# A perceiver layer on one core: the second attention with its last softmax in two halves, contiguous K for the content, staging slots renumbered, and V projections, transposes and products regrouped

## The chip, the core and the metric

The kernel runs on one core of a Trainium2 chip. A core has four compute engines and DMA queues, each with a program of its own: TensorE (PE) multiplies matrices into the eight banks of PSUM, VectorE (DVE) and ScalarE (ACT) work element by element and copy results out of PSUM, GpSimd (POOL) does the same on SBUF alone, and SyncE (SP) issues the transfers between DRAM and SBUF. They wait for one another only by semaphores. The metric is the device time of one execution in microseconds (us); lower is better.

## What is computed

Queries are x, 4 batches of 128 rows of 512 values (16 heads of 32), and a context of 2048 rows per batch. Three residual blocks follow one another, each behind a layer norm: a cross attention over the context (softmax over heads and batches), a self attention with relative positions, and a third attention with normalised queries and gates. The change lies in the second:

```python
q, k, v = (proj(Wq), proj(Wk), proj(Wv))
a_q = Eq[rel]; a_k = Ek[rel]; a_v = Ev[rel]         # rel: clipped distance of l and m
content = jnp.einsum('bhld,bhmd->bhlm', q, k)
rel_k = jnp.einsum('bhld,lmd->bhlm', q, a_k)
rel_q = jnp.einsum('bhmd,lmd->bhlm', k, a_q)
pos_pos = jnp.einsum('lmd,lmd->lm', a_q, a_k)
logits = (content + rel_k + rel_q + pos_pos) * scale
attn = jax.nn.softmax(logits, axis=-1)
out = jnp.einsum('bhlm,bhmd->bhld', attn, v) + jnp.einsum('bhlm,lmd->bhld', attn, a_v)
```

All of it is float32. Projections are made of three products of rounded parts ("hi" and "lo"), twelve matmuls of 512 columns for one 128 x 512 result.

## The kernel before

The code is written by hand, engine by engine; the order in a function is the order on the engine, and every wait is written out. No scheduler moves anything.

The second attention works in four groups (`hg` or `u`, 0 to 3) of four heads, each over all four batches. For each group PE projects K (`keys2`) into bank 4 and Q (`queries2`) into bank 5, in two halves each, with the relative rows (`relative(n)`, 16 rounds, four a group: two for "rq", made of K, and two for "rk", made of Q) between them, in banks 0 to 3. ACT copies K and Q out of PSUM with row and batch exchanged (`k_lb`, `q_lb`: batch innermost, so that rows of all batches stand together for the relative products); one batch of `k_lb` is read with a step of four floats. DVE copies Q once more, contiguous (`q_rows`), from the same bank.

The relative rows are evacuated into six staging slots of the `blocks` buffer (`staged(n)`, DVE for rq, ACT for rk), stored by SP to DRAM (`rel_store`, 636 KB each) and read back with a skewed pattern that turns distances into columns (`rel_load`, 1210 KB each): `rq_in_u` and `rk_in_u`. SP's order is fixed: stores of the next group between the two loads of one. After them come the load of the third attention's Wq (`weight_load(4)`), of the table of values `EvRel`, and of its Wk (`weight_load(5)`, once POOL has done `weight_lo(4)`).

Then, for each group, PE writes the logits into banks 4 to 7: sixteen transposes of the rq part (L639) and sixteen matmuls of content over it (L644). DVE adds the rk part (`add2`, L1486) and takes maximum and difference (`softmax2`, L1490 and L1493); of group 3 it leaves the difference to ACT, which has the scaled maximum (L1496) as bias. ACT exponentiates (`exp2`; group 3 in sixteen instructions, L1078), PE transposes the probabilities (`attention_t(u)`, L663, groups 0 and 1 through banks 0 to 3, 2 and 3 through banks 4 to 7), and ACT (group 2: DVE, L1521) copies them into `probs_t(u)`, which shares the `blocks` buffer with the staging slots, so before the first of these copies ACT waits for all stores. V is projected by batch (`values2(b, bank)`, L381) through banks 0 and 1. PE multiplies attention and V (L704, sums in banks 0 to 3), ACT copies the results (L1115), PE puts them back transposed (L712), and the table of values follows in four banks of 64 matmuls' records (L724); DVE scales with the reciprocal sums and adds the residual (L1532, L1534), transposes the table part (L1540), POOL scales it (L1283), PE adds it (L741), and the third layer norm begins (`moments2`, square root on ACT at L873).

Weights of the third attention come in between: ACT rounds them (`weight_hi(n)`, L881) and POOL makes the low part (`weight_lo(n)`, L1217).

## Time and profile before

| | us |
|---|---|
| median of 3 runs | 748.01 |
| lowest and highest | 745.55, 748.47 |
| the profiled execution, its own time | 749.99 |
| its span | 748.0 |
| mean granted clock of PE | 0.993 |

The span is the time from the first to the last record of the profiled execution. Busy times of the page: PE 718.3, DVE 625.2, ACT 490.0, POOL 502.3 us. In the page's view in 40 slices, the DMA share of the slices between about 580 and 636 us is 9, and 4 or under nearly everywhere else behind the first slice. In this span the first attention lasts to about 567 us, the second from there to about 671, the third to the end. A busy share is a mean over these stages; each stage has limits of its own, and what a change in one is worth is read from the waits of that stage. "Idle before" in a row is the time in which the engine had nothing to do before it, and behind the arrow stands what released it; "issue" means that the profile shows no wait.

### The profile page before, as it was taken

Reading aid. Unit: us, or ns where it says so; the run is one execution under the profiler, and the core shown is the slowest. Engines: PE = TensorE matmul, PEld = TensorE weight load, DVE = VectorE, ACT = ScalarE, POOL = GpSimd, SP = SyncE. Lnnn points to the kernel's source line nnn. Section 1 sums busy time; section 2 is a strip of 40 time slices with the busy share of each in tenths; the row PEclk is TensorE's granted clock in tenths of the full one; section 3 lists DMA queues with packets and bytes.
Section 4 is the critical chain, followed back from the end, with each engine's and each line's share of the span. In section 5 each row is a group of like instructions: output and inputs, shape, how many; then the busy total and the mean of one; then the engine's idle time right before and its main releaser. Section 6 shows DMA issues by size and latency. Waiting matters only on the chain.

```text
span 748.0 us, 17289 instructions
## 1 busy us (share of the span) xinstructions
PE 718.3 (96%) x7542; PEld 572.1 (76%) x7542; DVE 625.2 (84%) x507; ACT 490.0 (66%) x694; POOL 502.3 (67%) x282
## 2 busy tenths in 40 slices
PE   8999999999999999999999999999988979889988
PEld 7777777777777777877778777787676667767876
DVE  5479999999999999999999999999946349767685
ACT  5578668777777867768677687767615444725681
POOL 0165979889898898989989898897962020243300
PEclk9999999999999999999999999999999999999999
DMA  8310110101101011010101101010013999420101
GB/s 330 115 58 6 53 57 2 58 1 58 57 2 58 1 58 39 19 58 3 57 7 53 57 2 58 1 58 2 1 57 112 337 391 362 172 100 1 57 2 57
DMA packets 15339, 55.71 MB, mean 74 GB/s; under 512 B 1696, under 2 KB 2080, under 8 KB 11680
## 3 DMA queue, kind: packets, MB, share of 16 engines
q1 hardware_dynamic: 15264, 54.61, 20.0%
q8 instruction: 60, 0.98, 0.6%
q14 instruction: 15, 0.12, 0.1%
HBM read 43.13 MB, written 11.47 MB: 73 GB/s over the span
## 4 chain that ended last, share of the span: by engine, by line
PE 81%; DVE 10%; ACT 5%; issue 3%; POOL 0%; ACTq 0%; DVEq 0%; POOLq 0%
PE ps L381 25%; PE ps L362 24%; PE ps L470 9%; PE ps L497 7%; PE ps L370 2%; PE ps L617 2%; PE ps L419 2%; DVE blocks L1476 1%; PE ps L724 1%; ACT v_buf L906 1%; DVE extra L1370 1%; DVE extra L1399 1%; DVE ps L1399 1%; PE ps L639 1%; PE ps L644 1%
## 5 line engine op out<-in xcount | busy, mean ns | idle before, releaser
L1239 POOL TENSOR_TENSOR s_buf<-s_buf,r_all 128x1024 f32<-128x1024 f32 x93 | 197.2, 2159 | 3.6 <-DVE r_all L1412 3.6
L930 ACT ACTIVATE s_buf<-s_buf 128x1024 f32<-128x1024 f32 x128 | 135.7, 1065 | 10.0 <-DVE s_buf L1392 9.1
L914 ACT COPY s_buf<-ps 128x1024 f32<-128x1024 f32 x128 | 123.3, 1018 | 20.4 <-PE ps L470 20.4
L1370 DVE TENSOR_REDUCE extra<-s_buf 128x128 f32<-128x2048 f32 x48 | 109.5, 2281 | 10.4 <-ACT s_buf L914 10.4
L1392 DVE TENSOR_TENSOR s_buf<-s_buf,ps 128x2048 f32<-128x2048 f32 x48 | 106.9, 2282 | 0.5
L1217 POOL TENSOR_TENSOR w_lo<-raw,w_hi 128x2048 fp32r<-128x2048 f32 x6 | 27.8, 4636 | 99.2 <-ACT w_hi L881 70.1
L906 ACT COPY v_buf<-ps 128x512 f32<-128x512 f32 x64 | 37.6, 588 | 77.5 <-PE ps L381 58.0
L1206 POOL TENSOR_TENSOR v_buf<-v_buf,extra 128x512 f32<-128x512 f32 x64 | 81.1, 1303 | 7.8 <-ACT v_buf L906 7.8
L1399 DVE TENSOR_REDUCE ps<-s_buf 128x128 f32<-128x4096 f32 x16 | 70.8, 4428 | 16.1 <-ACT s_buf L930 16.0
L1212 POOL TENSOR_TENSOR odd_lo<-extra,odd_hi 128x512 fp32r<-128x512 f32 x32 | 40.9, 1298 | 54.9 <-ACT odd_hi L889 54.9
L470 PE MATMUL ps<-q_t,k_t 32*128 32x128 f32 x2048 | 75.1, 283 | 2.4 <-ACT v_buf L906 0.9
L470 PEld LDWEIGHTS ps<-q_t,k_t 32*128 32x128 f32 x2048 | 63.3, 186 | 17.7 <-issue 17.7
L497 PE MATMUL ps<-s_buf,v_buf 128*32 128x128 f32 x2048 | 73.3, 283 | 3.5 <-DVE s_buf L1420 3.5
L497 PEld LDWEIGHTS ps<-s_buf,v_buf 128*32 128x32 f32 x2048 | 55.5, 110 | 27.2 <-issue 27.2
L1399 DVE TENSOR_REDUCE extra<-s_buf 128x128 f32<-128x2048 f32 x32 | 72.9, 2277 | 0.0
L1233 POOL TENSOR_TENSOR s_buf<-s_buf,m_all 128x2048 f32<-128x2048 f32 x16 | 66.1, 4134 | 2.7 <-DVE m_all L1385 2.7
L896 ACT ACTIVATE k_t<-ps,cols 128x512 f32<-128x512 f32 x64 | 44.2, 690 | 27.9 <-PE ps L362 27.2
L381 PE MATMUL ps<-w_hi,x_hi 128*128 128x512 f32 x176 | 48.1, 395 | 0.3 <-ACT x_hi L1022 0.3
L1212 POOL TENSOR_TENSOR x_lo<-raw,x_hi 128x512 fp32r<-128x512 f32 x28 | 35.8, 1305 | 18.3 <-ACT x_hi L889 18.3
L381 PE MATMUL ps<-w_lo,x_hi 128*128 128x512 f32 x176 | 47.1, 389 | 0.0
L381 PE MATMUL ps<-w_hi,x_lo 128*128 128x512 f32 x176 | 47.1, 389 | 0.0
L1370 DVE TENSOR_REDUCE ps<-s_buf 128x128 f32<-128x2048 f32 x16 | 36.7, 2296 | 9.7 <-ACT s_buf L914 8.1
(218 smaller groups left out, 1450.9 us busy)
## 6 DMA issues: line engine op xcount, KB each, us to landing
rel_scratch<-blocks SPq DMA_DIRECT2D x16, 636.0 KB, 10.9
s_buf<-rel_scratch SPq DMA_DIRECT2D x7, 1210.0 KB, 9.9
raw<-in_ctxT SPq DMA_DIRECT2D x8, 1024.0 KB, 4.8
extra<-in_ctxT SPq DMA_DIRECT2D x8, 1024.0 KB, 5.1
raw<-in_Wq SPq DMA_DIRECT2D x2, 1024.0 KB, 6.5
raw<-in_Wv SPq DMA_DIRECT2D x2, 1024.0 KB, 5.7
extra<-in_EvRel SPq DMA_DIRECT2D x1, 2048.0 KB, 12.6
extra<-rel_scratch SPq DMA_DIRECT2D x1, 1210.0 KB, 10.3
```

Of the source, the lines that this page charges most:

```text
L362: last = mm(ps[:, bank, :], w_parts[v][:, slot, c, hg * P:(hg + 1) * P], x_parts[u][:, c, :], start=n + c == 0, stop=n == 2 and c == C - 1)
L381: last = mm(ps[:, bank, :], x_parts[u][:, c, b * P:(b + 1) * P], w_parts[v][:, slot, c, :], start=n + c == 0, stop=n == 2 and c == C - 1)
L470: last = mm(pair, k_t[rows, w, keys], q_t[rows, w, keys], start=True, stop=True, skip_group_check=True)
L497: last = mm(ps[j * HD:(j + 1) * HD, bank, b * P:(b + 1) * P], v_of(t)[:, b, h * HD:(h + 1) * HD], probs[:, j, b // 2, :, b % 2], start=b = ...
L914: copy(piece(t, 2 * w + u).rearrange("p e (u n) -> p (e u) n", u=2), ps[:, 2 * u:2 * u + 2, :]).then_inc(s["s_evac"], 1)
L930: nc.scalar.activation(piece(t, p), piece(t, p), ACT.Exp).then_inc(s["exp_done"], 1)
L1206: pool.tensor_tensor(v, v, bv_all, ALU.add).then_inc(s["v_ready"], 1)
L1212: pool.tensor_tensor(lo[:, :, rows], raw_of(t)[:, :, rows], hi[:, :, rows], ALU.subtract).then_inc(s["ctx_lo"], 1)
L1239: pool.tensor_tensor(part, part, spread(r_all, 4), ALU.mult).then_inc(s["attn_pool"], 1)
L1370: nc.vector.tensor_reduce(m_ps if k == 0 else m_next[:, k % 2, :], over_pairs(t, 2 * k, 2), AX.XY, ALU.max).then_inc(s["max_done"], 1)
L1392: tt(part, part, m_wide.broadcast_to([P, 8, P, 2]), ALU.subtract).then_inc(s["sub_dve"], 1)
L1399: nc.vector.tensor_reduce(r_ps if k == 0 else z_next[:, k % 2, :], over_pairs(t, p, n), AX.XY, ALU.add).then_inc(s["sum_done"], 1)
```

## The change

Eight things, all but the last in the second attention:

1. DVE copies each group's K contiguous too (`key_rows`, into `v_buf[:, 1]`, ahead of the group's relative rows); the content matmuls read it instead of `k_lb`. The buffer is the one V goes to, so ACT's copy of V of batch 3 waits for the fourth logits.
2. In group 3 the Q copy stands between the two rq rounds; the first logits wait for it only at their last four transposes, since the four banks are taken in the order 0, 2, 3, 1.
3. The staging slots are shifted by two, so that the last rounds to be stored lie where the last probabilities go; each copy of transposed probabilities waits for its two slots only.
4. PE's order: transposes of group 0 stand ahead of the third logits, those of group 1 and V of batches 2 and 3 ahead of the fourth, attention times V of groups 0 and 1 ahead of the transposes of group 2.
5. The last softmax (addition, maximum, scaling) is done in two halves of two batches, and ACT's last exponentials in two eights behind them.
6. ACT's order follows PE's; its rounding of the third Wq (`weight_hi(4)`) moves behind all copies of probabilities.
7. POOL takes `weight_lo(5)` behind its four products.
8. Semaphores that count one thing each are merged in pairs (`m_done`, `r_done`, `soft_dve`, `soft_act`, `q3_rsp`); in the first and third attention nothing else changes.

```diff
@@ slots and buffers
+        def k_rows(hg):
+            return v_buf[:, 1, hg, :]
         def staged(n):
-            base = n % SLOTS * 2 * ROWS
+            base = (n + 2) % SLOTS * 2 * ROWS
+        def slot_landed(engine, *slots):
+            for slot in slots:
+                n = (slot - 2) % SLOTS
+                engine.wait_ge(s[f"rel_out_{n}"], 16 * len(range(n, NROUND, SLOTS)))
@@ PE
                 if k == 0 and hg > 0:
                     pe.wait_ge(s["kf_evac"], hg)
+                    pe.wait_ge(s["kr_evac"], hg)
...
             def values2(b, bank):
-                if b < 2:
+                if b == 0:
                     pe.wait_ge(s["rk_evac"], 2 * C)
                 else:
-                    pe.wait_ge(s["at_done"], B + b - 1)
+                    pe.wait_ge(s["at_done"], (2, B + 1, B + 2)[b - 1])
...
             def logits(u):
                 if u == 0:
-                    pe.wait_ge(s["kf_evac"], C)
-                    pe.wait_ge(s["qr_evac"], C)
+                    pe.wait_ge(s["kr_evac"], C)
...
-                for j in range(J):
+                for j in (0, 2, 3, 1):
+                    if u == 0 and j == 1:
+                        pe.wait_ge(s["qr_evac"], C)
...
-                                  k_lb[rows, u, :, b], start=False, stop=True, skip_group_check=True)
+                                  k_rows(u)[rows, b * P:(b + 1) * P], start=False, stop=True, skip_group_check=True)
...
             def attention_t(u):
                 if u == 0:
-                    pe.wait_ge(s["v2_evac"], 2)
+                    pe.wait_ge(s["v2_evac"], 1)
                 elif u == 2:
-                    pe.wait_ge(s["lg_done"], C)
+                    pe.wait_ge(s["lg_done"], C + 1)
                 for b in range(B):
                     if u == 1:
                         pe.wait_ge(s["at_done"], b + 1)
+                        if b == 1:
+                            pe.wait_ge(s["v2_evac"], 2)
...
+            pe.wait_ge(s["v2_evac"], B)
+            pe.wait_ge(s["at_done"], 2 * B)
+            attend2(0)
+            attend2(1)
+            attention_t(2)
+            attention_t(3)
+            pe.wait_ge(s["at_dve"], B)
+            attend2(2)
+            attend2(3)
@@ ACT
             def values2(b, bank):
                 act.wait_ge(s["v2_psum"], b + 1)
+                if b == C - 1:
+                    act.wait_ge(s["lg_psum"], C)
...
             def exp2(u):
                 for b in range(B):
+                    if b % 2 == 0:
+                        act.wait_ge(s["sub2"], C + b // 2)
@@ POOL
-            pool.wait_ge(s["sub2"], C)
+            pool.wait_ge(s["sub2"], C + 1)
             weight_lo(4)
-            weight_lo(5)
             pool.wait_ge(s["rinv2"], 1)
             for b in range(B):
...
+            weight_lo(5)
@@ DVE
+            def softmax2_last(n):
+                u = C - 1
+                part = heads(rk_part(u))[:, 2 * n:2 * n + 2]
+                tt(part, ps[:, 4:8, :].rearrange("p j (b m) -> p b j m", b=B)[:, 2 * n:2 * n + 2], part,
+                   ALU.add).then_inc(s["lg_done"], 1)
+                dve.wait_ge(s["lg_done"], C + n)
+                top = rmax[:, u * H + 8 * n:u * H + 8 * n + 8]
+                nc.vector.tensor_reduce(top, lg(u)[:, 8 * n:8 * n + 8], AX.X, ALU.max).then_inc(s["max2"], 1)
+                dve.wait_ge(s["max2"], C + n)
                 nc.vector.tensor_scalar(top, top, -SCALE, None, ALU.mult).then_inc(s["sub2"], 1)
...
+            def key_rows(hg):
+                dve.wait_ge(s["kf_evac"], hg + 1)
+                nc.vector.tensor_copy(k_rows(hg), ps[:, 4, :]).then_inc(s["kr_evac"], 1)
...
             for hg in range(C):
+                key_rows(hg)
                 relative(4 * hg)
+                if hg == C - 1:
+                    query_rows(hg)
                 relative(4 * hg + 1)
-                query_rows(hg)
+                if hg < C - 1:
+                    query_rows(hg)
...
             total2(0)
-            add2(3)
-            softmax2(3)
+            dve.wait_ge(s["lg_psum"], C)
+            dve.wait_ge(s["rk_in_3"], 16)
+            softmax2_last(0)
+            softmax2_last(1)
+            slot_landed(dve, 3, 4)
```

On PE, before, this stands from the first transposes of probabilities (L663) on: L639 and L644 are logits, L381 a third of a V projection, L704 attention times V.

```order
632 L663 MATMUL ps<-ident,s_buf 128x128 x16
633 L639 MATMUL ps<-ident,s_buf 128x128 x16
634 L644 MATMUL ps<-v_buf,s_buf 128x128 x16
635 L663 MATMUL ps<-ident,s_buf 128x128 x32
636 L381 MATMUL ps<-w_hi,x_hi 128x512 x4
637 L381 MATMUL ps<-w_lo,x_hi 128x512 x4
638 L381 MATMUL ps<-w_hi,x_lo 128x512 x4
639 L381 MATMUL ps<-w_hi,x_hi 128x512 x4
640 L381 MATMUL ps<-w_lo,x_hi 128x512 x4
641 L381 MATMUL ps<-w_hi,x_lo 128x512 x4
642 L663 MATMUL ps<-ident,s_buf 128x128 x16
643 L704 MATMUL ps<-blocks,v_buf 32x128 x64
```

And now, from the second transposes of probabilities on (L675; logits L649 and L654, V L389, attention times V L709):

```order
633 L675 MATMUL ps<-ident,s_buf 128x128 x16
634 L389 MATMUL ps<-w_hi,x_hi 128x512 x4
635 L389 MATMUL ps<-w_lo,x_hi 128x512 x4
636 L389 MATMUL ps<-w_hi,x_lo 128x512 x4
637 L389 MATMUL ps<-w_hi,x_hi 128x512 x4
638 L389 MATMUL ps<-w_lo,x_hi 128x512 x4
639 L389 MATMUL ps<-w_hi,x_lo 128x512 x4
640 L649 MATMUL ps<-ident,s_buf 128x128 x16
641 L654 MATMUL ps<-v_buf,s_buf 128x128 x16
642 L709 MATMUL ps<-blocks,v_buf 32x128 x32
643 L675 MATMUL ps<-ident,s_buf 128x128 x32
644 L709 MATMUL ps<-blocks,v_buf 32x128 x32
```

The fourth logits moved from ahead of the second transposes and the last two V projections to behind them, and half of attention times V from the very end to ahead of the last 32 transposes.

On ACT, before, from the first copies of transposed probabilities (L1089) on; L1074 and L1078 are exponentials, L881 rounds a weight, L1069 copies V, L1115 copies attention times V:

```order
436 L1089 COPY blocks<-ps 128x512 x4
437 L1074 ACTIVATE s_buf<-s_buf 128x16x128
438 L881 CAST w_hi<-raw 128x2048
439 L1089 COPY blocks<-ps 128x512 x4
440 L1078 ACTIVATE s_buf<-s_buf,rmax 128x128 x16
441 L1069 COPY v_buf<-ps 128x512 x2
442 L1089 COPY blocks<-ps 128x512 x4
443 L1115 COPY k_t<-ps 128x512 x4
444 L881 CAST w_hi<-raw 128x2048
```

And now, from the second such copies (L1111) on; exponentials are L1091 and L1097, the rounding L896, V L1086, attention times V L1137:

```order
437 L1111 COPY blocks<-ps 128x512 x4
438 L1086 COPY v_buf<-ps 128x512
439 L1091 ACTIVATE s_buf<-s_buf 128x16x128
440 L1086 COPY v_buf<-ps 128x512
441 L1097 ACTIVATE s_buf<-s_buf,rmax 128x128 x16
442 L1111 COPY blocks<-ps 128x512 x4
443 L896 CAST w_hi<-raw 128x2048
444 L1137 COPY k_t<-ps 128x512 x4
445 L896 CAST w_hi<-raw 128x2048
```

The rounding of the third Wq moved from ahead of the second copies of probabilities to between the last of them and the copies of attention times V; both V copies stand ahead of the sixteen exponentials.

## Rows read from the trace of the kernel before

**Rows 1.** The page, part 1: busy time and share of the span.

```profile
PE 718.3 (96%) x7542; PEld 572.1 (76%) x7542; DVE 625.2 (84%) x507; ACT 490.0 (66%) x694; POOL 502.3 (67%) x282
```

**Rows 2.** Windows: busy time of PE, PEld, DVE, ACT, POOL, granted clock, DMA share, GB/s.

```profile
584.00:628.00 44.00, 39.87 (x392) 30.50 (x391) 25.56 (x22) 19.16 (x16) 4.56 (x1) 0.96 1.02 379
...
612.00:618.00 6.00, 4.66 (x44) 4.11 (x44) 5.93 (x3) 3.72 (x3) 0.00 (x0) 0.72 1.03 397
```

**Rows 3.** DMA issues at 615.66 and 645.47: start, duration; size, us to landing.

```profile
615.66 0.36 SPq L257 DMA_DIRECT2D s_buf<-rel_scratch  x1
s_buf<-rel_scratch SPq DMA_DIRECT2D x1, 1210.0 KB, 9.9
...
645.47 0.33 SPq L257 DMA_DIRECT2D raw<-in_Wk  x1
raw<-in_Wk SPq DMA_DIRECT2D x1, 1024.0 KB, 5.0
```

**Rows 4.** Timeline of DVE: start, us, instruction, count, idle before and releaser.

```profile
606.74 0.68 DVE L1504 COPY s_buf<-ps 128x512 f32<-128x512 f32 x1
...
611.58 2.29 DVE L1486 TENSOR_TENSOR s_buf<-ps,s_buf 128x2048 f32<-128x2048 f32 x1 [4.16 <-PE ps L644]
...
626.61 2.29 DVE L1486 TENSOR_TENSOR s_buf<-ps,s_buf 128x2048 f32<-128x2048 f32 x1
...
635.91 2.29 DVE L1486 TENSOR_TENSOR s_buf<-ps,s_buf 128x2048 f32<-128x2048 f32 x1 [0.18 <-PE ps L644]
...
640.64 2.48 DVE L1521 COPY blocks<-ps 128x512 f32<-128x512 f32 x4
...
643.03 6.66 DVE L1500 TENSOR_REDUCE rsum<-s_buf 128x16 f32<-128x2048 f32 x3
```

**Rows 5.** Timeline of PE, the same columns, of the same stretch.

```profile
607.57 1.94 PE L639 MATMUL ps<-ident,s_buf 128*128 128x128 f32 x16 [2.36 <-DVE s_buf L1504]
...
613.39 1.44 PE L617 MATMUL ps<-tab,k_t 32*128 32x159 f32 x16 [1.34 <-ACT blocks L1065]
...
614.77 2.91 PE L639 MATMUL ps<-ident,s_buf 128*128 128x128 f32 x16
...
647.44 3.14 PE L704 MATMUL ps<-blocks,v_buf 128*32 128x128 f32 x105
...
652.17 0.75 PE L704 MATMUL ps<-blocks,v_buf 128*32 128x128 f32 x20 [1.60 <-issue]
...
657.21 7.20 PE L724 MATMUL ps<-blocks,extra 128*32 128x64 f32 x192
```

**Rows 6.** Timeline of ACT, the same columns.

```profile
618.55 1.92 ACT L1074 ACTIVATE s_buf<-s_buf 128x2048 f32<-128x2048 f32 x1 [1.13 <-DVE s_buf L1493]
...
641.09 4.81 ACT L1078 ACTIVATE s_buf<-s_buf,rmax 128x128 f32<-128x128 f32 x16
...
645.79 1.05 ACT L1069 COPY v_buf<-ps 128x512 f32<-128x512 f32 x2
...
646.73 2.06 ACT L1089 COPY blocks<-ps 128x512 f32<-128x512 f32 x4
...
654.14 2.02 ACT L881 CAST w_hi<-raw 128x2048 fp32r<-128x2048 f32 x1
...
656.17 1.28 ACT L873 ACT_TABLE_LOAD   x1
...
668.59 0.29 ACT L873 ACTIVATE rstd<-mean_var,gtmp 128x1 f32<-128x1 f32 x1 [11.13 <-DVE mean_var L1302]
```

**Rows 7.** Chain of waits: start, us, engine, tile and line.

```profile
609.50 2.00 PE ps L644 x32
...
626.43 2.96 PE ps L381 x12
...
695.92 1.10 PE ps L786 x32
```

**Rows 8.** Timeline of POOL, columns as of DVE.

```profile
640.81 4.64 POOL L1217 TENSOR_TENSOR w_lo<-raw,w_hi 128x2048 fp32r<-128x2048 f32 x1 [29.05 <-DVE rmax L1496]
```

100 lines of the change are left out of this document (45 added, 55 removed).

## The prediction

> **What bounds the kernel now.** I read the views in this order: the page, the windows, the timelines of the engines, the DMA issues, and last the chain of waits. The page shows TensorE (PE) busy for 96% of the span [rows 1]. That average covers a long first stage that the change leaves alone but for names of semaphores. The edits lie between 568 and 669 us, in the second attention, and there PE isn't the only limit. From 584 to 628 us the 16 DMA engines are busy for a share of 1.02 and move 379 GB/s [rows 2]: they write the relative rows to DRAM and read them back skewed. The read of the third group's key part is issued at 615.66 and lands 9.9 us later, at 625.6 [rows 3]. VectorE's (DVE's) third addition starts at 626.61, so that transfer is only 1.0 us short of deciding it. DVE is nearly gapless from the first addition (611.58) to the last of the sums (649.7); before the fourth addition it waits 0.18 us, for PE [rows 4]. After that the end goes through ScalarE (ACT: sixteen exponentials, two V copies, four copies of transposed probabilities, the last done at 648.8) and PE, which starts all four groups of "attention times V" only at 647.44 and ends them at 653.0, with a stall of 1.60 us that no wait explains [rows 5, 6]. So what the stage is worth is read at that milestone: the end of attention times V, 653.0.
>
> **The change part by part.**
> *Copies and renumbering.* Four copies of K to a contiguous buffer are added on DVE, each like the Q copy at 0.68 us [rows 4], 2.7 us in all. Each stands ahead of its group's relative rows, where DVE waits for PE (between 584 and 628 it is busy 25.56 of 44 us [rows 2]), so it costs nothing; without that cover it would be 0.7 us a group on PE's next K projection. The merged semaphores wait for the same events: nothing. The six staging slots change places, not their cyclic use, and SP's queue issues the same DMAs in the same order, so the DMA stream stays as it is.
>
> *The first logits.* They wait no longer for the Q copy of the fourth group, which removes PE's idle 2.36 us [rows 5]; only the last four transposes wait for it, and it is made before the relative rows now. With contiguous K the 32 records of content should take the 1.10 us of the third attention's logits in place of 2.00 us [rows 7]. PE: free at 605.2, transposes 1.94, content 1.1, end 608.3 to 608.4. The first addition starts there, 3.2 us earlier than at 611.58. Most of it doesn't last: the second group of DVE's work (three instructions of 2.29 each) is over at 622.2, and the third addition must wait for the transfer of 625.6. At this point the gain is 1.0 us, and DVE idles 3.4.
>
> *PE's new order.* I add it up. The first subtraction ends at 615.3, exp takes 1.92, the first V copy half of the 1.05 that two take, and hand-overs some 0.3: at 618.05 PE starts the first transposes [rows 6]. Then it has no gap: two groups of transposes (2 x 1.94), two of logits (2 x 2.95), three V projections (3 x 2.96) [rows 5, 7], 18.7 us, so the fourth logits end at 636.9. Before, they ended at 635.9. The two V projections and the second transposes that stood behind them stand ahead of them now, and DVE waits about 2 us for them.
>
> *The last softmax in halves.* The full instruction is 2.29 us [rows 4], a half 1.2 (half the elements and a small fixed part), the scaling 0.17. First half ready at 639.5, second at 642.1. The first eight exponentials (of 4.81 for sixteen [rows 6]) run 639.5 to 641.9, the other eight 642.1 to 644.5. Before, they ended at 645.9, with V copies of 1.05 behind them, which come earlier now. DVE copies the third group's transposes in 2.48 by 644.6 [rows 4], the last PE transposes are hidden but for the last batch, and ACT's four copies take 2.06 [rows 6]: 646.6 in place of 648.8, a gain of 2.2.
>
> *Attention times V.* Two of its four groups (about 1.0 us each by the 3.14 for 105 of 128 records [rows 5]) are moved into the wait ahead of the third transposes, the third group waits only for DVE's copies, and behind the last ACT copy stands one batch, 0.3 us. The milestone goes from 653.0 to 647.0: 6.0, of which 2.2 are the softmax and 3.8 the moved work with the stall.
>
> *The moved weight work.* ACT's cast of the third Wq, 1.9 us, now stands right ahead of the four copies of attention times V. They run 648.6 to 650.7; PE has the first quarter of its table values to do from 647.0 (2.5 us, by 7.20 for three quarters [rows 5]) and then takes one copy each 0.5 us, so it waits at most 0.2. PE's last table values (7.20) end at 658.6 instead of 664.4: 5.8. DVE's three last sums (6.66 [rows 4]) and the reciprocal end at 651.8; the eight instructions behind them have the shape of the Q copy (0.68) and end near 657.4, still ahead. Behind the cast comes POOL's subtraction (4.64 [rows 8]), done at 653.5, then SP's load of the third Wk (5.0 [rows 3]), 658.7, ACT's cast (2.02) and the 1.28 us reload of its table, 662.0 [rows 6]. The first square root of the layer norm is due at 668.59 less 5.8, at 662.8: 0.8 us of room. POOL's other subtraction goes behind its four products and ends near 668.5, long before the keys of the third attention need it.
>
> Sum: 0 (copies) + 0 (first logits, eaten by the transfer) - 2.2 - 3.8 + 0.2 = -5.8. Steps I didn't see, such as a semaphore more on each hand-over, I put at 0.4: -5.4. The profiled execution took 749.99 (span 748.0), so its like would take 744.6; the median of the runs is 748.01, 1.98 less, which gives 742.6.
>
> Two things have no row of before. *Contiguous K*: bounds 1.10 and 2.00 us; I take 1.10, the same operation with the same shapes. At 2.00 three of the four logits are on the path, +2.7. *The clock of PE*: it ran at 0.72 of full speed between 612 and 618 [rows 2], that is part of the time at 1.2 GHz, after the two idle spells of 2.36 and 1.34 us, and sixteen transposes took 2.91 in place of 1.94, and the relative rows before them 1.44 [rows 5], of which 0.6 or so are the clock's: 1.6 us. The new order takes out 2.36 us of idle there, but adds 1.3 of waiting at 639.6 and small waits between batches up to 647. Bounds: one such drop less that shows, 0 (it is hidden behind the transfer), and one more on the path, +1.6. I take none.
>
> Here the Trainium skill speaks against the change. "TensorE: Matmul & The Clock Gate", Part 4 (PE-mode transpose), says that transposes don't count as busy for the clock gate as matmuls do. From 639.6 to 645.2 the new order has nothing but transposes; by that rule the drop would come there and cost about 1.6 by the rows at both levels, and the sum would be -3.8; without it -5.4. In the trace a stretch of idle and transposes from 605.3 to 609.5 stood before a drop that came some 4 us later, which fits either view, so I give it a chance and not the forecast. On the stall, "Runtime: NRT & Kernel Launch", Instruction fetch mechanics, says that the fetch of the next block is hidden by the issue of the current one. The row shows 1.60 us behind no wait, just after the Wk load of 645.47 was on the queues, so I don't trust it here; with fetch always hidden the new order loses no more, and a stall between 653.6 and 658.7 is excluded.
>
> **The rivals.**
> *Half clock once* (at 611 to 615 or at 640 to 650), price 1.6: 744.2. For it: idle of 1.3 at 609 and at 639.6. Against it: less idle in sum than before.
> *The moved weights or a stall decide.* The new Wk load goes out at 653.6, while PE runs through its table values fast. A stall as before (1.60), or a landing of 8 us instead of 5, delays the layer norm by 1.6 to 2.2: 744.5.
> *K is not faster contiguous*: +2.7, 745.3. The change then doesn't do there what it says. Against it, the two rows at 1.10 and 2.00.
> *The room is larger than I think* (no stall, and the logits meet DVE earlier): 740.7.
> *Slower than before: PE's chain from 618 to 637 at half clock.* It is gapless and DVE has only one waiting place behind it, so all of it counts: four transposing parts at +1.0, two of content at +1.1, three projections at +2.96, 15 us, 757.6. It decides from the point where 5.4 us are lost, a third of the chain at 1.2 GHz. Against it: PE always has work there, and the drop of before came after idle.
>
> **How the numbers follow.** Forecast 0.53, 742.6 (own range 741 to 744.3). Half clock once 0.19; weights or stall 0.12; K not faster 0.05; larger room 0.06; slower 0.05. Half a per cent, about what can be told from no change, is 3.7 us: faster means under 744.3. The forecast nearly all and the larger room are under it, half clock once by half, weights by a third: 0.71. Over 751.7 lies the slower rival, 0.05; the rest 0.24. The range goes from 740.4 (larger room) to 747.0 (K not faster and a half clock together, 746.9).
>
> **What would show it.** Content of the logits at 1.10 us a group instead of 2.00. First addition near 608.4, third near 625.6, released by a DMA. The fourth logits' end near 636.9 and DVE idle 2 us before it. Last ACT copy near 646.6, table values' end near 658.6, the first square root at 662.8 released by DVE. I am wrong if the first square root is released by the cast, if the clock falls after 618, or if the third addition waits for PE.

## The result, and the profile after

| | before | changed |
|---|---|---|
| median, us | 748.07 (6 runs) | 743.78 (6 runs) |
| lowest and highest | 745.55, 748.47 | 742.55, 745.07 |
| ratio, with its 95% interval | | 0.9932 (0.9914 to 0.9950) |
| the profiled execution, its own time | 749.99 | 745.07 |
| its span | 748.0 | 743.1 |
| mean granted clock of PE | 0.993 | 0.993 |

The changed kernel is 4.3 us faster by these medians, 0.6%. The ratio stands for 5.1 us (3.7 to 6.4), and the changed kernel run again beside 29 runs of before is 5.4 us below their median (e1), so the gain is about 4 to 5.5 us and not known finer than that. The forecast was 742.6 with a range of 740.4 to 747.0; the time lies in the range, 1.2 us above the forecast. The page of the changed kernel, part 1, answers to [rows 1]: PE 2 us less, DVE 3 us more (mostly the four copies), the rest as before. It tells no more than that.

```profile
PE 716.2 (96%) x7542; PEld 569.6 (77%) x7542; DVE 628.5 (85%) x514; ACT 490.5 (66%) x694; POOL 502.0 (68%) x282
```

Before milestones can be compared, the two traces need a common zero. The windows of the changed kernel (busy time of PE, PEld, DVE, ACT, POOL, granted clock, DMA share, GB/s) show one thing in the first attention, where nothing was changed:

```profile
80.00:100.00 20.00, 18.19 (x205) 14.23 (x204) 18.32 (x11) 13.26 (x16) 17.72 (x10) 0.91 0.01 2
...
584.00:628.00 44.00, 41.00 (x437) 31.28 (x437) 27.47 (x24) 22.69 (x22) 4.53 (x1) 1.00 1.01 373
...
638.00:642.00 4.00, 2.29 (x67) 2.05 (x68) 3.90 (x5) 1.92 (x7) 0.00 (x0) 1.00 0.96 406
642.00:646.00 4.00, 3.85 (x31) 3.04 (x29) 3.97 (x7) 3.86 (x13) 0.00 (x0) 1.00 0.02 8
...
662.00:666.00 4.00, 4.00 (x6) 1.35 (x5) 2.28 (x7) 0.97 (x3) 4.00 (x4) 0.59 0.21 80
```

And the same stretch of the kernel before:

```profile
80.00:100.00 20.00, 18.16 (x213) 14.27 (x214) 19.70 (x13) 14.66 (x18) 17.89 (x10) 1.00 0.01 2
```

In the changed kernel's profiled execution the clock fell to its lower level (1.2 GHz) for a short spell somewhere between 80 and 100 us, and a mean of 0.91 over 20 us is what such a spell leaves. So everything behind it is late, by 1.50 us where the last relative rows ahead of the first logits start, as the PE timelines show (start, us, instruction, count, idle before and releaser). The row of before:

```profile
604.39 0.82 PE L617 MATMUL ps<-tab,v_buf 32*128 32x159 f32 x16
```

And PE's rows of the changed kernel (L626 relative rows, L649 and L654 logits, L675 transposes of probabilities, L709 attention times V, L739 table values, L756 transposes back for the layer norm), which answer to [rows 5]:

```profile
605.89 0.82 PE L626 MATMUL ps<-tab,v_buf 32*128 32x159 f32 x16
606.64 1.97 PE L649 MATMUL ps<-ident,s_buf 128*128 128x128 f32 x16
608.54 1.17 PE L654 MATMUL ps<-v_buf,extra 32*128 32x128 f32 x32
...
619.30 1.94 PE L675 MATMUL ps<-ident,s_buf 128*128 128x128 f32 x16 [0.90 <-ACT v_buf L1086]
...
636.47 1.17 PE L654 MATMUL ps<-v_buf,s_buf 32*128 32x128 f32 x32
638.40 1.95 PE L709 MATMUL ps<-blocks,v_buf 128*32 128x128 f32 x64 [0.76 <-ACT v_buf L1086]
641.67 4.57 PE L675 MATMUL ps<-ident,s_buf 128*128 128x128 f32 x32 [1.31 <-DVE s_buf L1519]
646.17 1.96 PE L709 MATMUL ps<-blocks,v_buf 128*32 128x128 f32 x64
...
652.30 7.20 PE L739 MATMUL ps<-blocks,extra 128*32 128x64 f32 x192
661.60 4.65 PE L756 MATMUL ps<-v_buf,ident 128*128 128x512 f32 x6 [2.11 <-POOL v_buf L1304]
```

The wait of 2.36 us ahead of the first logits is gone, the content takes 1.17 us instead of 2.00, attention times V runs in two pieces of 64 without a stall, and what is left of the long wait for the last softmax is 1.31 us. DVE's rows, which answer to [rows 4]:

```profile
609.78 2.29 DVE L1508 TENSOR_TENSOR s_buf<-ps,s_buf 128x2048 f32<-128x2048 f32 x1 [0.68 <-PE ps L654]
...
626.64 2.29 DVE L1508 TENSOR_TENSOR s_buf<-ps,s_buf 128x2048 f32<-128x2048 f32 x1 [3.07 <-DMA s_buf<-rel_scratch]
...
637.71 1.23 DVE L1519 TENSOR_TENSOR s_buf<-ps,s_buf 128x1024 f32<-128x1024 f32 x1 [1.93 <-PE ps L654]
638.97 1.22 DVE L1523 TENSOR_REDUCE rmax<-s_buf 128x8 f32<-128x1024 f32 x1
```

The third addition is released by the DMA, as predicted, and the halves of the last softmax by PE. ACT's rows, which answer to [rows 6] (exponentials, copies of transposed probabilities, rounding of the third Wq, rounding of the third Wk, table reload, first square root):

```profile
640.43 5.04 ACT L1097 ACTIVATE s_buf<-s_buf,rmax 128x128 f32<-128x128 f32 x16 [2.08 <-DVE rmax L1525]
645.37 2.00 ACT L1111 COPY blocks<-ps 128x512 f32<-128x512 f32 x4
647.27 2.07 ACT L896 CAST w_hi<-raw 128x2048 fp32r<-128x2048 f32 x1
...
659.18 1.90 ACT L896 CAST w_hi<-raw 128x2048 fp32r<-128x2048 f32 x1 [7.87 <-DMA raw<-in_Wk]
661.10 1.28 ACT L888 ACT_TABLE_LOAD   x1
663.69 0.30 ACT L888 ACTIVATE rstd<-mean_var,gtmp 128x1 f32<-128x1 f32 x1 [1.30 <-DVE mean_var L1324]
```

The first square root is released by DVE and has 1.3 us of room. So the stage is read from one place to another: from the last relative rows ahead of the first logits to the end of the last table values (start plus duration of the row of 192). Before: 604.39 to 664.41 [rows 5], 60.0 us. Changed: 605.89 to 659.50, 53.6. From there to the end of the span it is 83.6 us in both. The profiled executions differ by 4.9 us: 6.4 won in the stage, 1.5 lost at 80 to 100 us.

Such spells can be counted. Each trace has from none to four of them, each seen as 0.91 in a window of 20 us, and the mean granted clock of the whole execution follows their number: about 0.998 with one, 0.995 with two, 0.993 with three, 0.991 with four (in e3 below one window of 0.83 counts for two). Runs without a trace have that mean too, so it tells how many spells a run had, though not where they lay.

### The profile page after: what moved, and what is told of

It reads as the page before. It is cut to its first block, busy times and chain, and to the rows that moved or that the text cites. A ratio compares the mean times of both kernels' runs of the same rounds, so it can differ in the third digit from the quotient of the medians.

```text
span 743.1 us, 17302 instructions
## 1 busy us (share of the span) xinstructions
PE 716.2 (96%) x7542; PEld 569.6 (77%) x7542; DVE 628.5 (85%) x514; ACT 490.5 (66%) x694; POOL 502.0 (68%) x282
## 4 chain that ended last, share of the span: by engine, by line
PE 80%; DVE 12%; ACT 5%; issue 3%; POOL 0%; ACTq 0%; DVEq 0%; POOLq 0%
PE ps L389 25%; PE ps L370 24%; PE ps L478 9%; PE ps L505 7%; PE ps L378 2%; PE ps L626 2%; PE ps L427 2%; DVE blocks L1498 1%; PE ps L739 1%; ACT v_buf L921 1%; DVE extra L1392 1%; DVE extra L1421 1%; DVE ps L1421 1%; PE ps L529 1%; DVE s_buf L1414 1%
## 5 line engine op out<-in xcount | busy, mean ns | idle before, releaser
L505 PEld LDWEIGHTS ps<-s_buf,v_buf 128*32 128x32 f32 x2048 | 55.6, 110 | 27.3 <-issue 27.3
L389 PE MATMUL ps<-w_hi,x_hi 128*128 128x512 f32 x176 | 48.1, 395 | 0.3 <-ACT x_hi L1037 0.3
L1234 POOL TENSOR_TENSOR x_lo<-raw,x_hi 128x512 fp32r<-128x512 f32 x28 | 35.8, 1303 | 18.3 <-ACT x_hi L904 18.3
L389 PE MATMUL ps<-w_lo,x_hi 128*128 128x512 f32 x176 | 47.1, 389 | 0.0
L389 PE MATMUL ps<-w_hi,x_lo 128*128 128x512 f32 x176 | 47.1, 389 | 0.0
```

Source lines behind the costliest of these rows:

```text
L389: last = mm(ps[:, bank, :], x_parts[u][:, c, b * P:(b + 1) * P], w_parts[v][:, slot, c, :], start=n + c == 0, stop=n == 2 and c == C - 1)
L505: last = mm(ps[j * HD:(j + 1) * HD, bank, b * P:(b + 1) * P], v_of(t)[:, b, h * HD:(h + 1) * HD], probs[:, j, b // 2, :, b % 2], start=b = ...
L1234: pool.tensor_tensor(lo[:, :, rows], raw_of(t)[:, :, rows], hi[:, :, rows], ALU.subtract).then_inc(s["ctx_lo"], 1)
```

## The experiments

Each ran beside runs of the kernel before on the same chip; ratios are against those, with 95% intervals. One chip ran e1 to e4, a second e5 to e8, a third e9 to e12. The kernel before has medians of 749.10, 748.61 and 748.74 us there, so differences from e1 of some tenths of a us mean little behind e4. Where "stage" stands with a number, it is the stretch just defined, in the profiled execution. In the expectations theory A is mine, B the rival; each says what it means there.

### e1: the changed kernel again

No edit. The question is whether the profiled execution of the changed kernel was typical, and what the clock's spells do.

> The changed kernel once more, unchanged, to see how much of its runs is chance. Its trace lost 6.4 us between the last relative rows before the first logits and the end of the table values, the medians only 4.3. Theory A (the stage is worth 6.4, the rest of the difference is the number of half-clock spells, which falls differently in every run): in the runs of both kernels the time goes with the mean granted clock, about 1.3 to 1.5 us for each 0.002 to 0.003 of it, and the profile again has the stage at 53.5 to 54 us. Theory B (the change gives back 2 us elsewhere): the third attention or the first is longer than before in every profile of the changed kernel, by 2 us.

Measured: 743.68 us (742.28 to 744.25), ratio 0.9928 (0.9912 to 0.9944). The profiled execution took 742.28, span 740.3, with a clock of 1.00 in the windows from 600 to 680 us. Its stage is 53.6 again. Its PE timeline at the place of the row at 661.60 above:

```profile
660.06 4.12 PE L756 MATMUL ps<-v_buf,ident 128*128 128x512 f32 x8 [2.10 <-POOL v_buf L1304]
```

Eight records here take 4.12 us; eight took 5.52 in the execution above (the chain of waits has 5.52 for all eight), where the clock was 0.59 from 662 to 666. The same wait of 2.1 us stands ahead of both, so the fall behind it comes in some executions and not in others, and it costs 1.4 us where it comes. Theory A holds for the stage and for the steps of time with the clock.

### e5: the kernel before again

No edit either. The stall of 1.60 us in [rows 5] is the largest thing in the forecast that no wait explains.

> The kernel before, unchanged, for a second trace of the stage. The first had a stall of 1.60 us that no wait explains in attention times V, and a half-clock spell from 613 to 617. At equal granted clock the runs of before are 3.3 (at 0.998) to 4.6 us (at 0.995) above those of the changed kernel, the traced stage 6.4. Theory A (stall and spell are chance events that only some executions have): the stage (last relative rows before the first logits to the table values' end) is 58 to 58.5 here if the stall is absent. Theory B (the stall is built in): 60 again, stall 1.5 to 1.7 at the same record.

Measured: 749.19 us in 8 runs (745.56 to 750.65), ratio 1.0003 (0.9983 to 1.0024). The profiled execution took 746.51 (span 744.5). Its PE timeline, first logits' transposes, attention times V, table values and the layer norm's transposes:

```profile
604.50 0.82 PE L617 MATMUL ps<-tab,v_buf 32*128 32x159 f32 x16
607.68 2.46 PE L639 MATMUL ps<-ident,s_buf 128*128 128x128 f32 x16 [2.36 <-DVE s_buf L1504]
...
647.13 3.70 PE L704 MATMUL ps<-blocks,v_buf 128*32 128x128 f32 x128
...
655.01 7.20 PE L724 MATMUL ps<-blocks,extra 128*32 128x64 f32 x192
664.31 4.11 PE L741 MATMUL ps<-v_buf,ident 128*128 128x512 f32 x8 [2.11 <-POOL v_buf L1283]
```

Attention times V is one piece of 128, with no stall. The stage is 604.50 to 662.21, 57.7 us. So 2.3 of the 60.0 of the first profile are not in every execution. From the start of attention times V to that of the last table values it was 9.77 us there and is 7.88 here, so 1.9 of the 2.3 lie at the stall and 0.4 ahead of it. This pair, e5 and e1, is the cleanest there is: neither has a fall of the clock at 660 to 680, both have 82.3 us from the table values to the end, and the relative rows start within 0.2 us of each other; e5 has one spell more, at 608 to 612 us, which only the old order has. Their spans differ by 744.5 - 740.3 = 4.2 us, their stages by 57.7 - 53.6 = 4.1.

### e2: content matmuls on the old K

```diff
-  k_rows(u)[rows, b * P:(b + 1) * P], start=False
+  k_lb[rows, u, :, b], start=False
```

> The changed kernel, but the content matmuls read K with its step of four floats again (the contiguous copies are still made). Theory A (the chain of PE from the first logits to the fourth decides, and content of groups 0, 2 and 3 is in it): content 2.00 us a group in place of 1.10, fourth logits 2.7 us later in the stage, median +2.7 (746.5). Theory B (DVE and the transfers hide PE, only the fourth is on the path): +0.9 (744.7).

Measured: 746.87 us in 12 runs, ratio 0.9971 (0.9960 to 0.9983), 3.2 us slower than e1. PE's timeline:

```profile
604.55 0.82 PE L626 MATMUL ps<-tab,v_buf 32*128 32x159 f32 x16
...
607.20 2.07 PE L654 MATMUL ps<-v_buf,extra 32*128 32x128 f32 x32
...
619.62 1.94 PE L675 MATMUL ps<-ident,s_buf 128*128 128x128 f32 x16 [0.77 <-ACT v_buf L1086]
...
637.68 2.09 PE L654 MATMUL ps<-v_buf,s_buf 32*128 32x128 f32 x32
```

From the relative rows to the first transposes of probabilities it is 15.1 us here and 13.4 in the changed kernel: the first two contents are both on the path, since the V projection stands behind the second and the transposes wait for its V copy. On ACT that copy now waits 0.64 us for the projection; in the changed kernel it runs straight behind the exponential. To the end of the fourth content it is 35.2 against 31.75, 3.5 us for four contents of 0.9 each. The prediction had three of the four on the path.

### e10: contiguous K alone, on the kernel before

```diff
+            def key_rows(hg):
+                dve.wait_ge(s["kf_evac"], hg + 1)
+                nc.vector.tensor_copy(k_rows(hg), ps[:, 4, :]).then_inc(s["kr_evac"], 1)
...
             for hg in range(C):
+                key_rows(hg)
                 relative(4 * hg)
```

(and the content matmuls read `k_rows`.)

> The kernel before with one part of the change: K copied contiguous and read so by the content matmuls; nothing else. Undone in the changed kernel this part cost 3.2 us. Theory A (in the old order the transfers and DVE hide it except at the fourth logits, which wait for their transfer anyway): the traced stage is 0.9 shorter than the 57.7 without stall, at equal clock the runs are 0.5 to 1.2 lower (747.5 to 748.5 in median). Theory B (worth the same everywhere): -3.2.

Measured: 747.88 us in 12 runs, ratio 0.9995 (0.9980 to 1.0009): 0.4 us, and at most 1.5 by the interval. That excludes theory B's 3.2; by the medians it is 0.9, inside theory A's band, so a small gain is not excluded. The last three contents do take 1.17 us (the first, in the spell of low clock, takes 2.09). But the stage is 603.33 to 661.85, 58.5 us: longer than e5's 57.7 and not 0.9 shorter, as theory A had it. PE's timeline shows where it went:

```profile
627.38 1.94 PE L667 MATMUL ps<-ident,s_buf 128*128 128x128 f32 x16 [1.09 <-ACT v_buf L1073]
631.19 1.97 PE L643 MATMUL ps<-ident,s_buf 128*128 128x128 f32 x16 [1.87 <-DMA s_buf<-rel_scratch]
```

And DVE's at the last addition:

```profile
634.53 2.29 DVE L1490 TENSOR_TENSOR s_buf<-ps,s_buf 128x2048 f32<-128x2048 f32 x1 [0.42 <-DMA s_buf<-rel_scratch]
```

PE is early and waits 1.87 us for the fourth group's transfer, and DVE needs it too. The relative rows start 1.2 us earlier than in e5 and the fourth logits' transposes 0.35 us earlier (631.19 against 631.54). The edit that is worth 3.2 us in the new order is worth little or nothing in the old one: the old order puts the fourth logits where only a transfer can be waited for, the new one has two V projections and a group of transposes there.

### e3: the last softmax whole

```diff
-            softmax2_last(0)
-            softmax2_last(1)
+            softmax2_whole()
```

(`softmax2_whole` does one addition, maximum and scaling of all four batches and counts each semaphore up by 2.)

> The changed kernel, but the last addition, maximum and scaling are whole (2.29, 2.29, 0.17) as before. Theory A: the first exponential starts at about +2.1 and the last ACT copy of probabilities ends 1.9 later, median +1.9 (745.7). Theory B (the halves win nothing, since all sixteen exponentials must be over): +0 to +0.3.

Measured: 746.40 us in 12 runs, ratio 0.9967 (0.9950 to 0.9983), 2.7 us slower than e1. PE's timeline of the last transposes of probabilities and of attention times V:

```profile
643.35 0.71 PE L675 MATMUL ps<-ident,s_buf 128*128 128x128 f32 x4 [1.93 <-ACT s_buf L1097]
644.51 3.42 PE L675 MATMUL ps<-ident,s_buf 128*128 128x128 f32 x12 [0.46 <-ACT s_buf L1097]
647.87 3.26 PE L709 MATMUL ps<-blocks,v_buf 128*32 128x128 f32 x64
```

And two of its windows:

```profile
644.00:646.00 2.00, 1.46 (x7) 1.06 (x7) 2.00 (x2) 2.00 (x8) 0.00 (x0) 0.50 0.00 0
...
648.00:650.00 2.00, 2.00 (x40) 1.85 (x43) 2.00 (x2) 2.00 (x3) 0.00 (x0) 0.50 0.04 8
```

Two things are in the 2.7. The wait for ACT is longer: against runs of the changed kernel at the same mean clock e3 is 1.6 us slower at 0.995 (745.3 to 743.73) and 2.1 at 0.998 (744.51 to 742.41), about the 1.9 to 2.2 of the softmax term. And behind that wait the clock falls to 0.50, in the middle of the path. Of the 12 runs 6 have a mean clock of 0.991, a value that no run of the changed kernel has.

### e4: attention times V all at the end

```diff
-            attend2(0)
-            attend2(1)
             attention_t(2)
             attention_t(3)
+            attend2(0)
+            attend2(1)
             pe.wait_ge(s["at_dve"], B)
```

> The changed kernel, but attention times V of groups 0 and 1 stands behind all transposes again. Theory A: +1.9 (745.7), the work of 64 pairs that no wait hides any longer; a further 1.6 if the stall behind no wait comes back with it (it needs a load on the queues at that moment, and the load of Wk goes out only at 654 now, so I expect no stall). Theory B (the products are hidden by the last ACT copies): +0 to +0.4.

Measured: 746.35 us in 12 runs, ratio 0.9968 (0.9953 to 0.9984), 2.7 us slower than e1. PE's timeline:

```profile
641.59 5.35 PE L675 MATMUL ps<-ident,s_buf 128*128 128x128 f32 x32 [4.02 <-DVE s_buf L1519]
646.87 3.70 PE L709 MATMUL ps<-blocks,v_buf 128*32 128x128 f32 x128
```

And the window over the transposes:

```profile
642.00:646.00 4.00, 4.00 (x23) 4.00 (x22) 3.84 (x7) 3.51 (x12) 0.00 (x0) 0.57 0.06 20
```

The moved half takes 1.95 us and is back behind the transposes (3.70 instead of 1.96 there). At the same mean clock e4 is 1.2 (0.995) to 1.9 us (0.993, where the changed kernel has two runs) slower than the changed kernel. The rest is again a fall of the clock, behind an idle time of 4.0 us instead of 1.3. There is no stall in the row of 128, so the stall isn't tied to attention times V standing in one piece either.

### e6: the old slot numbers

```diff
-            base = (n + 2) % SLOTS * 2 * ROWS
+            base = n % SLOTS * 2 * ROWS
...
-                n = (slot - 2) % SLOTS
+                n = slot
```

The waits are by slot, so each copy still waits for the stores out of the two slots that it overwrites.

> The changed kernel with the staging slots numbered as before; each copy of probabilities still waits for its two slots alone. Theory A (late stores hold slots 0 and 1): the first copies of probabilities wait for the store of round 13 (issued 1.4 us later than before, landing near 16 to 17 us behind the first addition's start) and the second ones for round 15; they end 1.5 to 3 us later, PE's next V projections wait, median +1.5 to +2.5 (745.2 to 746.2). Theory B (the waits by slot are what counts, not the numbering): +0.

Measured: 744.14 us in 7 runs, ratio 0.9946 (0.9927 to 0.9965), 0.5 us slower than e1 by the medians and 1.3 by the ratios, less than expected. ACT's timeline, copies of transposed probabilities:

```profile
620.70 2.05 ACT L1111 COPY blocks<-ps 128x512 f32<-128x512 f32 x4 [4.42 <-DMA rel_scratch<-blocks]
...
627.50 2.06 ACT L1111 COPY blocks<-ps 128x512 f32<-128x512 f32 x4 [2.03 <-DMA rel_scratch<-blocks]
```

The mechanism is there: both copies wait for a store to DRAM, and PE waits 0.61 and 1.03 us behind them. The stage is 55.6 us, 2.0 more. But the median understates it. Four of the seven runs have a clock of 0.998 and one 1.0, where the changed kernel has mostly 0.995; at 0.998 the medians are 744.03 and 742.41, 1.6 us apart, at 0.995 there is one run (744.47), 0.7 over the changed kernel's 743.73. Renumbering is worth between 0.7 and 2.0 us. That is an estimate, since the two kernels ran on different chips and e6's interval overlaps e1's; 1.6 is my reading.

### e7: the fourth logits one projection earlier

```diff
             values2(2, 0)
-            values2(3, 1)
             logits(3)
+            values2(3, 1)
```

> The changed kernel with the fourth logits ahead of the last V projection instead of behind it. DVE waits 1.93 us for them now. Theory A (that wait is on the path): they must wait for their transfer, 1.2 us of idle on PE, and end 1.4 us earlier; the last V copy then delays ACT's exponentials by 0.7, so the last copy of probabilities ends 0.7 earlier: median -0.7 (743.0). Theory B (the gap moves to PE, and the later V projection delays attention times V): +0 to +1.

Measured: 742.11 us in 6 runs, ratio 0.9917 (0.9897 to 0.9938), 1.6 us below e1, but on another chip; the ratios are 0.8 us apart and their intervals overlap. At 0.998 of mean clock it is 0.4 faster (742.0 to 742.41), and the stage is 53.1, 0.5 less: about the 0.7 expected. The rest is the number of spells (4 of 6 runs have 0.998, of the changed kernel's 12 two). PE's timeline:

```profile
632.07 1.97 PE L649 MATMUL ps<-ident,s_buf 128*128 128x128 f32 x16 [1.13 <-DMA s_buf<-rel_scratch]
```

And DVE's:

```profile
635.36 1.23 DVE L1519 TENSOR_TENSOR s_buf<-ps,s_buf 128x1024 f32<-128x1024 f32 x1 [0.40 <-DMA s_buf<-rel_scratch]
```

DVE's wait of 1.93 us for PE turns into one for the transfer of the fourth group. The transfer is the next bound, as in e10, and gives the gain its ceiling.

### e8: something to do in PE's last wait

The wait of 2.1 us ahead of the layer norm's additions, which both kernels have, is one behind which the clock sometimes falls. Two matmuls with a zero weight (the upper right quarter of the identity) fill part of it; they add zero to the first of the sums.

```diff
             def table_values(b):
                 pe.wait_ge(s["av2_done"], b + 1)
+                if b == 0:
+                    for _ in range(2):
+                        mm(ps[0:64, 0, :], ident[0:64, 64:P], x_res[0:64, 0, :], start=False, stop=False,
+                           skip_group_check=True)
```

> The changed kernel with two matmuls that add zero to the first sum (a block of zeros of the identity by the residual) in PE's wait of 2.1 us ahead of the four additions of the table part. In most runs the clock falls to half there: the eight records take 5.52 us, and 4.12 in a run in which it didn't. Theory A (the fall follows from that idle): the records take 4.1, the granted clock of the runs rises from 0.995 to 0.998, median -1.2 (742.5). Theory B (the fall comes whatever PE does in these 2 us, or follows from the weak work ahead of it): +0, clock as before.

Measured: 741.74 us in 4 runs, ratio 0.9912 (0.9889 to 0.9935), 1.9 us below e1, on another chip. All four runs have a clock of 0.997 or more. PE's timeline:

```profile
657.86 1.93 PE L757 MATMUL ps<-x_res,ident 64*64 64x512 f32 x4
659.95 4.20 PE L760 MATMUL ps<-v_buf,ident 128*128 128x512 f32 x8 [0.16 <-POOL v_buf L1308]
```

The wait of 2.1 us becomes one of 0.16, nothing starts later, and the eight records take 4.20 us. That the filling keeps the clock up is not shown. Of the twelve traces without it five have the fall behind this wait and seven have not, so that the two traces with it (here and e9) have none can be chance. And on the chip of e8 the kernels without it have 0.998 or more in 9 of 13 runs too (e6 and e7).

### e9: e7 and e8 together

> The changed kernel with both edits: fourth logits ahead of the last V projection (stage 0.5 us shorter in its trace) and the two matmuls of zero in the wait ahead of the four additions (records 4.2 in place of 5.5). Theory A (the two add up, -0.5 and about -1.3): 741.2 to 741.5, granted clock 0.997 to 1.0. Theory B (the early logits helped only by a clock that didn't fall, which the matmuls do as well): the same as with the matmuls alone, 741.7.

Both diffs above. Measured: 741.56 us in 6 runs (739.79 to 743.23), ratio 0.9914 (0.9897 to 0.9931). The profiled execution took 739.79, with a clock of 1.0 over the whole span; its stage is 52.5. It is the lowest median of all the kernels here, 7.2 us below the runs of before on its chip, but its median is only 0.2 us from e8's and its interval overlaps e7's and e8's, so that the two gains add is not shown by the times.

### e11: the rounding of the weight behind the copies

```diff
             at_copy(3)
-            weight_hi(4)
             for b in range(B):
                 act.wait_ge(s["av2"], b + 1)
                 copy(k_t[:, b, :], ps[:, b, :]).then_inc(s["av2_evac"], 1)
+            weight_hi(4)
```

> The changed kernel with ACT's rounding of the third Wq behind the four copies of attention times V instead of ahead of them. Theory A (the chain rounding, POOL's low part, load of Wk, rounding of Wk, table reload has 1.3 us of room before the first square root of the layer norm): it goes out 2.5 to 3 us later and the square root waits for it, table values end 0 to 0.3 earlier, layer norm 1.2 to 1.8 later, median +1.2 to +1.6 (745.0). Theory B (the copies on ACT were held up by the rounding): -0.3.

Measured: 744.37 us in 6 runs, ratio 0.9955 (0.9941 to 0.9969), 0.7 us slower than e1, on another chip; 1.2 to 1.6 were expected. ACT's timeline:

```profile
661.10 1.90 ACT L896 CAST w_hi<-raw 128x2048 fp32r<-128x2048 f32 x1 [10.49 <-DMA raw<-in_Wk]
663.01 1.28 ACT L888 ACT_TABLE_LOAD   x1
664.31 0.29 ACT L888 ACTIVATE rstd<-mean_var,gtmp 128x1 f32<-128x1 f32 x1
```

The stage is the same (53.6), and the first square root now starts right behind the table load, with no wait for DVE. The first rounding starts 2.3 us later in the stage, the second, behind POOL and the load, 2.85 us later. That uses up the 1.3 us of room, and the first square root comes 1.55 us later. Little of it is left at the end: from the table values to the end of the span it is 83.9 us, against 83.6 in the changed kernel's first trace, where the clock falls at the same place. So the rival "moved weights decide" is real as a mechanism, and in the changed kernel it is 1.3 us away.

### e12: the Wk load out of the stall's neighbourhood

```diff
+            sp.wait_ge(s["av2"], B)
             weight_load(5)
```

(on the kernel before.)

> The kernel before, but SP issues the load of the third Wk only when attention times V is done (653 instead of 645.5). Its landing (about 658) is still 9 us ahead of the layer norm. Theory A (the stall of 1.60 us is a fetch of instructions held up by that load, in some executions): no run has it, the runs at equal clock lie together within 1 us (they spread over 2 to 3 us in the kernel before), median -0.8 to -1.6. Theory B (the stall has to do with something else): spread and median as before, +-0.3.

Measured: 748.22 us in 12 runs, ratio 0.9985 (0.9968 to 1.0003). The profiled execution has no stall, but neither have e5 and e10, which leave the load where it was. The interval touches 1, and the median is 0.5 us below that of before, less than theory A's 0.8 to 1.6. One forecast of theory A did come true: at equal mean clock the runs lie together within 1 us (six at 0.993 from 748.13 to 749.02, three at 0.998 from 745.14 to 745.40), while the kernel before on the same chip spreads over 2.4 us at 0.993 (eight runs) and 2.3 at 0.995 (seven). That speaks for the load, with few runs and no trace of a stall that went away. Inconclusive: neither that the load causes the stall nor that it doesn't is shown.

## Why the prediction was right, step by step

The range, the sign and the mechanism held; the forecast was 1.2 us low, and why is only in part settled. Milestones of the changed kernel, less the 1.5 us by which its trace is late:

| step | predicted | measured |
|---|---|---|
| content of the logits, a group | 1.10 | 1.17 |
| first addition of DVE | 608.4 | 608.3 |
| third addition, released by the DMA | 625.6 | 625.1 |
| fourth logits' end, DVE idle before it | 636.9, 2 | 636.1, 1.93 |
| last copy of probabilities ends | 646.6 | 645.9 |
| attention times V ends | 647.0 | 646.6 |
| table values end | 658.6 | 658.0 |
| room before the first square root | 0.8 | 1.3 |

**Chains.** All points in time came within 0.8 us, and all a little early. The addition of PE's instructions from 618 to 637 was the part that carried the forecast, and it held: from the first transposes to the end of the fourth logits it was 18.7 us by the prediction's sum (18.85 by its two times) and 636.47 + 1.17 - 619.30 = 18.3 measured. The slower rival (that chain at half clock) had nothing in it: every window from 602 to 662 shows 1.00. One of the prediction's own signs of being wrong did come, a fall of the clock after 618: it is the 0.59 at 662 to 666. But the first trace of before has the same fall (5.52 us for the same eight records), so it is no loss by the change, and the sign was drawn too wide.

**The stall: the doubtful term.** "Attention times V" was put at -3.8 us, of which 1.6 were the stall of [rows 5]. That stall isn't in e5, e10 or e12, which all keep the old order there. The forecast took off the 1.6 and then also the 1.98 us by which the profiled execution was over the median. If the median execution has no stall, it was subtracted twice: without it the term is -2.2 and the forecast 744.2, against 743.78 and 743.68 measured. For this reading speaks the pair of traces without it, 57.7 - 53.6 = 4.1, against 60.0 - 53.6 = 6.4 with it, and the 4.3 us between the first medians.

It is not the only reading. The 748.01 from which the forecast subtracts was the median of three runs. All the runs of before together (78 with the experiments, six with the result, on all chips) have 748.6, and the twelve of the changed kernel 743.7: 4.9 us, near the 5.4 of the forecast. And more than the clock varies in the kernel before. At 0.995 its 24 runs go from 745.56 to 749.52, the changed kernel's eight from 742.92 to 743.87, and the two executions of the old order that were traced at 0.995 and have no stall (746.51 in e5, 746.17 in e10) lie 1.4 and 1.8 us below the 747.95 of that group. A stall in a part of the runs would do that; no trace shows how often it comes.

At the same mean clock the kernels differ by 4.2 us (0.995: 747.95 in 24 runs, 743.73 in 8), 4.0 (0.993: 748.64 in 31, 744.66 in 2) and 3.2 (0.998: 745.66 in 2, 742.41 in 2). This compares unlike things a little: all four traces of the old order have one spell at 600 to 620 us, where it costs little, and the new order at the same mean has one more elsewhere, at up to 1.5 us. So these differences are probably too small.

**Contiguous K: right value, wrong size.** 1.10 us was the right end of the bounds. The price of the other end was put at 2.7 us and is 3.2 by the times and 3.5 by the stage (e2), since all four contents are on the path, the first two through the V copy that the first transposes wait for. The prediction looked for the first logits' effect on DVE alone, where the transfer eats it. It had the V copy start straight behind the exponential, which is so in the changed kernel, but with slow contents PE gets to that V projection late and the copy waits for it (0.64 us in e2).

**The softmax in halves: right.** -2.2 us was forecast, 1.6 to 2.1 at equal clock measured (e3), from one to two runs each.

**The moved products: right in kind.** 2.2 us forecast, 1.2 to 1.9 at equal clock measured (e4).

**Renumbering: not priced.** The prediction says that the DMA stream stays as it is, which is so, and puts no price on the slots. They have one: in the new order ACT's copies come earlier and would wait for the stores (e6, about 1.6 us). It isn't a gain over the kernel before, it is a loss that the change avoids. Of item 3 of the change only the numbering was undone, not the wait by slot.

**The parts don't add.** 3.2 + 2.7 + 2.7 + 0.5 is over 9 us for a change worth 4 to 5.5. Each part's price holds with the others in place: the order gives PE other work where a transfer is late, so that faster content counts, and K alone is worth 1.5 us at most (e10).

**The clock.** Transposes follow a wait of 1.31 us at 641.67, and the clock stays at 1.00 through the windows to 646: the rival "half clock once" didn't happen there. The Trainium skill ("TensorE: Matmul & The Clock Gate", Part 4, PE-mode transpose) has transposes not counting as busy for the clock in the way that matmuls do; here 4.57 us of them, 32 records of 128x128, went by at full clock, behind 1.95 us of products and the wait. With 4.0 us of idle in front instead of 1.3 (e4), or with 1.93 and 0.46 (e3), the clock did fall. That agrees with the rule in direction; that transposes alone bring the fall is not shown by the changed kernel. What the new order does for the clock in all is visible in the runs: of 78 runs of the kernel before 20 have a mean of 0.991 or less, and of 12 of the changed one none. Part of it has a place: in the four traces of the old order (before, e5, e10, e12) the first logits' transposes behind the 2.36 us of idle take 1.94 to 3.42 us and the windows of 600 to 620 show 0.91; in the ten traces of the changed kernel and its variants, where the idle is gone, none does. The price of this fall was small: the fourth addition starts 31.1 to 31.5 us behind the last relative rows in all four. The transfer doesn't hide all of it, as the prediction had it: in e5 and e12 DVE's third addition starts without a wait, 0.5 and 2.0 us behind the transfer's landing.

**What stays open.** The cause of the stall of 1.60 us and how often it comes. "Runtime: NRT & Kernel Launch" of the Trainium skill, Instruction fetch mechanics, has the fetch of instructions hidden by their issue. Whether the stall is such a fetch no run here shows: it is in one trace of the old order, three others don't have it, and no run is shown to make it come or go. Not tried alone are the early Q copy (item 2), the place of the first transposes of probabilities ahead of the third logits (item 4) and `weight_lo(5)` behind the products (item 7).

## What to carry to other kernels

Don't subtract a stall that no wait explains as a property of the code before a second profile shows it, and not on top of the difference to the median; and take that median from more than three runs, here 748.01 of three against 748.6 of all. Price a part within the order in which it will stand, since an edit that only makes an engine early at a transfer is worth nothing there and full price once other work fills the place. Compare runs at the same mean clock, but ask first whether the spells lie at the same places, and look at what follows each idle time of PE: 2 us of products moved into a wait were worth 2.7 us here (e4), part of it through the clock. Filling a wait with matmuls that add zero cost nothing (e8); that it helps isn't shown.

## What the hardware showed that I had not expected

- A fall of the clock comes or not behind the same wait: 2.10 us of idle ahead of the eight layer norm records, which then took 4.12 us in e1, 4.11 in e5 and 5.52 in the changed kernel's first profile. Each such spell shows as 0.91 in a window of 20 us, as 0.002 to 0.003 of the mean clock, and as 1.2 to 1.5 us of time where it is on the path. The spread of the times of the kernel before, from 745.5 to 752.3 us, goes along with that count in part: medians 745.66 at 0.998, 747.95 at 0.995, 748.64 at 0.993, 750.09 at 0.991, but up to 4.0 us within one of these groups.
- 32 content matmuls (weights 32x128, fp32) take 2.07 to 2.10 us with K read at a step of four elements and 1.17 with K contiguous, everywhere they stand at full clock (e2 and the changed kernel). The copies that make it contiguous take 2.7 us of DVE, and no wait of PE in the changed kernel's trace is put down to them; no run takes them out alone.
- The skewed reads of 1210 KB land at the pace of the full queues (window 584 to 628: DMA share 1.01, 373 GB/s), so once PE and DVE are reordered the fourth group's transfer ends the gain: 1.87 us of waiting in e10, 1.13 in e7.
